# The normalisation of the embedded block, moved behind the routing steps and the weight piece

## What is computed

```python
tokens = jnp.einsum('npd,hd->nph', p, W) + b          # + class token, + pos_embed
# local attention, 12 heads of 16, each query sees keys within 6 positions of the same image
qkv = (x @ w_qkv).reshape(B, N, 3, H, D)
p = jax.nn.softmax(scores, axis=-1); out = einsum('bnhw,bnwhd->bnhd', p, v_win); out @ w_proj + b_proj
# 8 experts, the two best of softmax(flat @ router_w.T), their weights normalised to sum 1
h = gelu(flat @ w1[e] + b1[e]);  out = out + w_e * (h @ w2[e] + b2[e])
```

## Time and profile before

| | |
|---|---|
| median of 3 runs | 1540.63 us (1539.32 to 1543.39) |
| the profiled execution | 1542.81 us |
| its span | 1540.9 us |
| mean granted TensorE clock | 0.981 |
| TensorE busy (PE) | 1422.7 us, 92% |
| VectorE busy (DVE) | 1105.3 us, 72% |
| ScalarE busy (ACT) | 664.2 us, 43% |
| GpSimd busy (POOL) | 900.0 us, 58% |

### The profile page before, as it was taken

The page is one execution under the profiler, slowest core; times in us unless marked ns, Lnnn a source line. Parts: engine busy times, 40 slices in busy tenths (PEclk is TensorE's granted clock), DMA queues, the critical chain, the costliest instruction groups (busy, mean ns, idle before and its releaser), DMA issues.

```text
span 1540.9 us, 51189 instructions
## 1 busy us (share of the span) xinstructions
PE 1422.7 (92%) x17688; PEld 1181.5 (77%) x17689; DVE 1105.3 (72%) x2824; ACT 664.2 (43%) x1148; POOL 900.0 (58%) x899
## 2 busy tenths in 40 slices
PE   4899999999999999999788899999999999999995
PEld 4788888888888888888566667777777777777774
DVE  2578888888888888788676686666666666666663
ACT  2455455454554555454445343333333333333331
POOL 4236566566665666565445776656666665665565
PEclk9999999999999999999899999999999999999998
DMA  5565565756675675755445475555555555555552
GB/s 168 173 191 151 160 194 152 208 155 188 164 197 142 171 202 145 201 159 137 103 87 95 74 155 75 76 73 74 77 73 73 74 74 73 75 74 73 73 73 31
DMA packets 305662, 189.18 MB, mean 123 GB/s; under 512 B 201977, under 2 KB 291397, under 8 KB 304477
## 3 DMA queue, kind: packets, MB, share of 16 engines
q1 hardware_dynamic: 241706, 118.06, 31.2%
q0 software_dynamic: 41680, 41.84, 18.4%
q10 hardware_dynamic: 22115, 27.08, 5.6%
HBM read 89.79 MB, written 65.29 MB: 101 GB/s over the span
## 4 chain that ended last, share of the span: by engine, by line
PE 56%; DVE 16%; POOL 11%; issue 8%; ACT 3%; ACTq 2%; DMA 2%; SPq 1%; another core or an unknown queue 1%; DVEq 0%; POOLq 0%
PE scores L1094 7%; PE qk L1109 7%; PE qk L1110 7%; PE qk L1111 7%; POOL sorted_scratch L501 5%; PE near L1094 5%; PE far L1094 3%; PE mixed L1094 3%; PE token_bank L1094 3%; PE qk L1205 3%; DVE qk L995 3%; PE near L1142 3%; POOL payload L513 2%; POOL os L538 2%; PE far L1218 2%
## 5 line engine op out<-in xcount | busy, mean ns | idle before, releaser
L501 POOL DMA_INDIRECT sorted_scratch<-payload,place x212 | 224.3, 1058 | 56.7 <-issue 56.3
L1142 PE MATMUL near<-we,both_patches 128*120 128x192 f32 x1272 | 224.1, 334 | 19.8 <-DMA both_patches<-in_xt 12.1
L1142 PEld LDWEIGHTS near<-we,both_patches 128*120 128x120 f32 x1272 | 208.2, 186 | 30.1 <-issue 28.2
L486 POOL DMA_INDIRECT out<-both_patches,token x111 | 203.7, 1835 | 37.4 <-issue 37.4
L486 POOL DMA_INDIRECT out<-v_side,token x108 | 200.2, 1854 | 37.7 <-issue 37.1
L576 ACT ACTIVATE stage<-near,bias 128x384 f32<-128x384 f32 x103 | 59.9, 581 | 360.4 <-PE near L1094 334.0
L1109 PE MATMUL qk<-w_hi,stage 128*128 x666 | 164.2, 247 | 2.8 <-DVE v_side L914 2.8
L1109 PE MATMUL qk<-w_hi,both_patches 128*128 x648 | 160.0, 247 | 5.2 <-issue 4.4
L1111 PE MATMUL qk<-w_hi,we 128*128 x666 | 164.2, 246 | 0.0
L1110 PE MATMUL qk<-w_lo,stage 128*128 x666 | 164.2, 246 | 0.0
L1111 PE MATMUL qk<-w_hi,both_patches 128*128 x648 | 159.9, 247 | 0.0
(11 more groups left out here) (259 smaller groups left out, 3689.3 us busy)
## 6 DMA issues: line engine op xcount, KB each, us to landing
both_patches<-in_xt SPq DMA_DIRECT2D x53, 720.0 KB
v_diag<-v_scratch SPq DMA_DIRECT2D x159, 89.2 KB
v_scratch<-v_side SPq DMA_DIRECT2D x53, 191.2 KB, 3.3
tabs<-tab_scratch SPq DMA_DIRECT2D x53, 180.0 KB
out<-h ACTq DMA_DIRECT2D x52, 180.0 KB
stage<-in_w ACTq DMA_DIRECT2D x8, 1152.0 KB
k_diag<-qk SPq DMA_DIRECT2D x436, 15.8 KB
stage<-in_w ACTq DMA_DIRECT2D x8, 576.0 KB
```

Of the source, the lines that this page charges most:

```text
L486: pool.indirect_dma_start(out=out, out_offset=bass.IndirectOffsetOnAxis(ap=token[k][:, n:n + 1], axis=0), in_=y[k % 2][:, n, :], in_offset ...
L501: pool.indirect_dma_start(out=sorted_dram, out_offset=bass.IndirectOffsetOnAxis(ap=at, axis=0), in_=payload[0:rows, 2 * (block % RING) + n ...
L1142: ins = pe.matmul(near[0:ROWS, n * D:n * D + D], patches[f % 2][:, x, n * ROWS:n * ROWS + ROWS], we[:, x, :], start=(x == 0), stop=(x == K ...
```

## The change

`normalise` of block t, with its two waits (for `rs1` of this block and for `lo1` of the one before), stands in VectorE's stream behind the weight splits of t = 0, routing parts 2 and 3, the table steps of t = 49 and 51 and the weight piece, and ahead of routing part 0. No other stream is touched.

```diff
@@ -953,8 +953,6 @@
                                       ALU.add).then_inc(s["h1_set"], 1)
                     dve.wait_ge(s["h1_set"], f + 1)
                     statistics(h1[f % H_RING], st1, mv1, "1", f + 1)
-                if runs(t, 0):
-                    normalise(h1[f % H_RING], mv1, rs1, xn1, "1", f + 1)
                 if t == 0:
 
                     for n, name in enumerate(weights32):
@@ -986,6 +984,8 @@
                         ins = dve.scalar_tensor_tensor(out=w1s[1][:, e, piece, :], in0=stage1[:, piece, :], scalar=WS, in1=w1s[0][:, e, piece, :],
                                                        op0=ALU.mult, op1=ALU.subtract)
                     ins.then_inc(s["split_lo"], 1)
+                if runs(t, 0):
+                    normalise(h1[f % H_RING], mv1, rs1, xn1, "1", f + 1)
                 if due_0:
                     route_steps(grp_0, 0)
                 if runs(t, 1):
```

## The result

The changed kernel takes **1516.1 us** (median of 4 runs, 1511.54 to 1520.12) against 1542.01 for the kernel before in the same session (4 runs, 1539.32 to 1547.4): ratio 0.9828, 95% interval 0.9801 to 0.9854. Run again later it gave 0.9870 (0.9825 to 0.9914). The forecast was 1522.5, range 1515 to 1537. So it is faster, by 20 us in one session and 26 in the other, where the sum said 18. The profiled execution took 1519.48 us, 23.3 less than that of before.

The account below looks back on a forecast made before the run. TensorE, busy 13 or more of about 14 us per iteration, was taken as nearly the bound. Terms 14 + 2 + 1 + 2 - 1 = 18 us gave 1524.8 from the profiled 1542.8, 1522.5 from the median; range 1515 to 1537.

Parts of the forecast that it names:

- the sum: Whole kernel: 14 + 2 + 1 + 2 - 1 = 18 us saved.
- The even iterations: From t = 8, routing fills the wait for `rs`; 14 odd iterations gain 1.0 us each: 14 us, bounds 7 and 17.
- t = 52: Last iteration with routing due, leading into a stage where VectorE's chain is alone: its 1.1 us counts whole, 1 us.
- The start: At t = 0 the weight splits and `bp` run ahead of `normalise`: 2 us saved, bounds 0 and 2.4.
- a wait for patches: Sign that the forecast is wrong, if such a wait appears; no size given.
- The odd iterations: Weight pieces move into the wait, only lengthening that for the logits: zero saved, late pieces lose 1 us, bounds 0 and 3.
- Slower: Rival: in odd iterations a piece holds L491 back, delaying `rs`, scatters and L531; +8 us, 1548.5, chance 0.05.
- The tables: At t = 49 and 51 the table steps go into the wait: 2 us saved together, bounds 0 and 3.
- the rival at 1530.5: GpSimd's two short steps hold up routing, leaving 0.5 us per even iteration: 11 us less 1; chance 0.17.
- More than the sum: Rival: three falls of the granted clock, 1.7 us each, may go with the waits; 1517.5, chance 0.12.
- the wait before `normalise`: Sign on VectorE: this wait goes from 72 us over the whole run to below 25.
- L790: Sign on VectorE: the wait before this line grows; no size given.

Follow-up runs that it names:

- Experiment 1: The kernel before, with `normalise` moved late only in the even iterations with routing due, from t = 8; 0.9909 of the kernel before, -14.0 us.
- Experiments 4: The changed kernel, but in even iterations `normalise` stands between routing parts 2 and 3; 0.9946 of the kernel before, -8.3 us.
- experiment 5: The whole change run again, against the kernel before; ratio 0.9870, -20.0 us.
- experiment 10: The changed kernel, but in even iterations `normalise` stands behind the low half of q and k and its copies; 0.9879 of the kernel before, -18.6 us.
- experiment 3: The kernel before, with `normalise` moved late at t = 0 only; 0.9981 of the kernel before, -2.9 us.
- Experiments 8: The changed kernel, with ScalarE's two expert weight issues moved behind the exponential for all experts but the first; 0.9841 of the kernel before.
- experiment 11: The kernel before, with only ScalarE's two expert weight issues moved behind the exponential for experts after the first; 0.9988 of the kernel before, -1.8 us.
- experiment 12: The changed kernel with ScalarE's expert weight issues moved behind the exponential, run a second time; 0.9833 of the kernel before, median 1514.31 us.

## Why the prediction came out right, point by point

**The even iterations: right in mechanism and size.** In iteration 36 routing starts at 501.17 right behind the aggregation, none of its steps is stretched, L995 starts 0.98 us earlier, and the odd iterations pay out: 12.7 us between the means of the profiles, where the forecast took 14. Experiment 1 measured 14.0 us for the 15 that the forecast gives this part with t = 52; the interval is 9 to 19. Experiments 4, 5 and 10, all with the late start, bracket it: stall partly filled, 8 us; filled, 20; `normalise` later than needed, 19. So the filled stall is what pays, and standing later still adds nothing that can be measured.

Two details came otherwise. The forecast priced a wait that goes at little more than its own length; in iterations 8 to 51 TensorE's idle time fell by 10.4 us and the time by 18.0. And L1066 did not lose its waits in the odd iterations: for `payload` and for ScalarE's L626 together they were 6.9 us before and 6.2 after, though those of L1172 went from 11.0 to 1.2. The odd iterations take 13.4 us on average, from 14.2, not 13.

**The start: right**, 1.9 us in the profile up to iteration 2, 2.9 (-0.6 to 6.5) in the runs, 2 forecast, and ended by the patches. The forecast named a wait for patches also as a sign that it is wrong. That wait came (4.64 us), but at 22.04, where the forecast had the embedding start anyway.

**The odd iterations: the number was right, the reason wrong.** "So the saved time only lengthens that wait: zero". The wait for the logits did not grow (15.7 us in odd iterations before, 14.9 with the pieces alone); VectorE and GpSimd held each other up instead, and the stall for `rs` shrank by 9.4 us where the pieces brought some 20. In the whole change the logits' wait even fell, to 8.1 us: TensorE is earlier, so the logits are.

**L491 behind the piece** was the mechanism of the rival *Slower*. L491 starts on time, 0.08 us behind the aggregation, but ends 0.6 us late, and that rival needed more than 1.4 us before GpSimd's L531 was moved. In iteration 35 GpSimd stands idle 1.32 us before L531. The place was right, the point from which it decides wasn't reached.

**The tables: 2 us forecast, 0.2 slower measured**, with bounds of 4 us either way; iteration 50 lost its wait, but the term is unproved.

**Routing beside L491 and L494** (the rival at 1530.5) fell. L810, with `chosen` and `tmp` as inputs, lies at 502.01 wholly within L494's 501.61 to 502.34 and takes its 0.19; 13 steps of L810 lie so within an L494 in the changed kernel, and its mean stays 192 ns. Only L812 grew, from 171 to 227 ns on average, 1.3 us over 23 iterations: seven of its steps take about 0.35 us, and each of these lies beside the end of a GpSimd scatter (L501), not beside L491 or L494. The Trainium skill (SBUF — State Buffer, Who interferes with whom) has a VectorE instruction with two SBUF inputs and a GpSimd one that reads SBUF exclude each other, whoever came first holding on to its end. L491 behind the piece agrees with it to 0.07 us; L810 within L494 does not, and there the trace decides.

**A term that was missing: the clock, in part.** The sum of 18 us stopped short of 20 to 26; the first session's 1516.1 lies nearest to the rival *More than the sum* (1517.5, chance 0.12), in which falls of the granted clock to half (1.2 of 2.4 GHz), 1.7 us each, go with the waits. In the block iterations before there are three such, after one (iteration 8, 0.90 above, behind a wait of 1.67 us), in experiment 5 one that cost 3.4. Over all runs the mean granted clock was 0.9815 with `normalise` early in the even iterations (128 runs) and 0.9842 with it behind routing part 2 or later (53 runs). Within the kernels, runs with a clock higher by 0.001 were 1.5 us faster (181 runs, correlation -0.72), so an estimate from these two numbers is 4 us.

But most of what the clock costs lies elsewhere: in the 14 profiles the falls cost 0 to 6.8 us in iterations 8 to 51, and 14.9 to 23.9 us from iteration 52 on, where the edit does next to nothing. The profiles show 1.7 to 3.4 us of clock gained in the block iterations (after and experiment 5 against before), and even that is within what kernels of one kind differ by: 0 to 6.8 us in the five with `normalise` early.

So the clock belonged in the forecast's sum with some 2 to 4 us, argued from these numbers and not shown by an experiment, since the clock can't be set; what else made the difference between 18 and 20 to 26 stays open, and 18 is inside the second session's interval (13 to 27).

**What did not come as foretold** besides L790: the wait before `normalise` went from 72.3 us over the whole run to 26.4 (28.0 in experiment 5), just not below 25; and there is a wait for the counts (L806, 11.7 us in 10 iterations). It costs nothing by itself, as VectorE there waits for the engine that bounds; but it marks the iterations in which something else (the weight issues) is late.

## What to carry to other kernels

When one engine waits at a fixed place in every turn, look for work behind it that needs nothing from what it waits for, and move it into the wait; price it by what the bounding engine waits for in the *next* turn, which may be of the other parity. Read such gains from many runs: sections with the same code differed by 10 us between profiles. Before moving work into a stall, ask which engine must run there to end the stall, and whether the work holds it up: sixteen small steps did not, one step of a microsecond did. And when stops before a busy engine go, its clock may give something back as well: look where its falls lie before counting them.

## What was not expected of the hardware

- **One stop of TensorE and then half the clock.** In iterations 7 to 51 of the 14 profiles, 630 in all, 19 have a mean clock below 0.96. Each of them holds a wait of TensorE of 1.3 to 2.6 us (in one case 0.91), 18 of them before the exponentials' turn L1172, 12 of them in iterations 8, 14, 20, 26, 32 and 44, in which ScalarE issues weights. Not every such wait does it, and not even most: 44 of the 630 iterations hold one of 1.3 us or more, and in 26 of these the clock stays full, as in iteration 44 of the changed kernel with 1.83 us (1.00 above). Most drops cost 1.7 us, as the earlier trace rows; the longest, iteration 14 of experiment 3, behind 1.88 us, turned 14 us into 20:

```profile
187.20:207.50 20.30, 18.42 (x230) 16.38 (x226) 13.45 (x49) 8.00 (x15) 9.58 (x13) 0.75 0.71 207
```

- **A short GpSimd step is stretched fourfold by a long vector step that starts 0.17 us ahead of it** (L491, 0.20 to 0.82 us), and the short routing steps leave it at 0.20; the one beside it, L807, reads only one input from SBUF, so this says nothing of a short step with two beside L491.
- **Waits shift rather than go.** Experiments 8, 11 and 12 took 7 to 8 us off TensorE's waits for the exponentials, and the time fell by 2 to 6 us against the kernel without that edit (8 and 12 against experiment 5, 11 against before), each time inside the intervals.
